# A 4x4 grid of convolution cells: the third of four copies of a last-column stream moves from VectorE to GpSimd

## What is computed

```python
def _cell(w, bias, ins):            # ins padded with zeros to 48 channels
    y = lax.conv_general_dilated(concatenate(ins, axis=1), w, (1, 1), 'SAME', ...)
    y = jax.nn.relu(y + bias[None, :, None, None])
    right, up, down = jnp.split(y, 3, axis=1)
    return (right, up, down)
for col in range(4):
    for row in range(4):
        if col == 0:   ins = [x] if row == 0 else [outs[row - 1][-1]]
        elif row == 0: ins = [outs[row][0], outs[row + 1][1]]
        elif row == 3: ins = [outs[row][0], outs[row - 1][-1]]
        else:          ins = [outs[row][0], outs[row + 1][1], outs[row - 1][-1]]
        outs[row] = _cell(W[col, row], b[col, row], ins)
return outs[-1][0]
x = x + grid(_gn(x), L0); x = x + conv(_gn(x)); x = x + gates(_gn(x)); x = x + grid(_gn(x), L3)
```

## Time and profile before

| | us |
|---|---|
| median of 3 runs | 434.03 (434.0 to 434.24) |
| the profiled execution, whole | 435.94 |
| its span, first to last instruction | 434.1 |
| PE busy | 403.1 (93%) |
| DVE busy | 301.6 (69%) |
| ACT busy | 199.4 (46%) |
| POOL busy | 205.2 (47%) |

### The profile page before, as it was taken

The page is one execution under the profiler, slowest core; times in us unless marked ns, Lnnn a source line. Parts: engine busy times, 40 slices in busy tenths (PEclk is TensorE's granted clock), DMA queues, the critical chain, the costliest instruction groups (busy, mean ns, idle before and its releaser), DMA issues.

```text
span 434.1 us, 12447 instructions
## 1 busy us (share of the span) xinstructions
PE 403.1 (93%) x5149; PEld 202.5 (47%) x5149; DVE 301.6 (69%) x563; ACT 199.4 (46%) x307; POOL 205.2 (47%) x384
## 2 busy tenths in 40 slices
PE   8999998989999897985998899999999999997884
PEld 5444444445554444543444455445444554444442
DVE  5789967537975346679587789968645954539684
ACT  7555533545526336465201455533545325347363
POOL 6277657955647433300000267657965594442300
PEclk9999999999999998999798999999999999998999
DMA  6076587868879665520000066588677797551701
GB/s 230 13 248 139 130 189 200 190 129 191 186 148 172 130 143 95 122 43 2 1 2 2 12 175 144 127 201 194 155 152 153 142 182 138 98 98 39 111 2 50
DMA packets 27304, 52.90 MB, mean 122 GB/s; under 512 B 11632, under 2 KB 13296, under 8 KB 27248
## 3 DMA queue, kind: packets, MB, share of 16 engines
q1 hardware_dynamic: 14416, 30.24, 30.8%
q0 software_dynamic: 12544, 21.14, 23.4%
q10 hardware_dynamic: 288, 0.72, 0.4%
HBM read 12.81 MB, written 0.52 MB: 31 GB/s over the span
## 4 chain that ended last, share of the span: by engine, by line
PE 57%; POOL 14%; DMA 11%; DVE 8%; ACT 5%; issue 3%; SPq 0%; DVEq 0%; ACTq 0%
PE bank L554 38%; PE bank L598 18%; POOL inp L534 11%; DMA inp<-cell_out 10%; POOL shifts L524 3%; ACT act_out L787 2%; DVE cell_out L1006 2%; DVE inp L718 1%; DVE inp L973 1%; DMA raw<-weights_in 1%; ACT cell_out L781 1%; ACT inp L718 1%; DVE inp L725 1%; DVE stat L860 1%; PE bank L617 1%
## 5 line engine op out<-in xcount | busy, mean ns | idle before, releaser
L534 POOL DMA_DIRECT2D inp<-cell_out x320 | 169.0, 536 | 142.1 <-DVE cell_out L1006 139.1
L787 ACT ACTIVATE act_out<-bank,bias 128x512 f32<-128x512 f32 x160 | 105.3, 687 | 101.3 <-PE bank L598 58.0
L554 PE MATMUL bank<-inp,w_heavy 128*32 128x512 f16 (+1 forms) x1536 | 139.8, 384 | 4.9 <-DMA inp<-cell_out 2.5
L1006 DVE TENSOR_TENSOR cell_out<-act_out,cell_out 128x512 f16<-128x512 f32 x156 | 107.8, 695 | 51.0 <-ACT act_out L787 47.0
L554 PE MATMUL bank<-inp,w_light 96*32 96x512 f16 (+2 forms) x1440 | 119.4, 395 | 12.8 <-DVE inp L973 10.3
L554 PEld LDWEIGHTS bank<-inp,w_heavy 128*32 128x32 f16 (+1 forms) x1536 | 65.1, 102 | 71.0 <-issue 13.8
L554 PEld LDWEIGHTS bank<-inp,w_light 96*32 96x32 f16 (+2 forms) x1440 | 59.8, 104 | 70.7 <-issue 19.8
L781 ACT ACTIVATE cell_out<-bank,bias 128x512 f16<-128x512 f32 x56 | 38.9, 694 | 87.0 <-PE bank L554 64.6
L598 PE MATMUL bank<-cell_out,w_first 32*128 32x512 f16 x1296 | 72.1, 378 | 0.0
L524 POOL DMA_DIRECT2D shifts<-inp x48 | 29.6, 623 | 59.0 <-DMA inp<-cell_out 58.8
L1000 DVE CAST cell_out<-act_out 128x512 f16<-128x512 f32 x100 | 42.9, 429 | 14.2 <-ACT act_out L787 13.5
(11 more groups left out here) (53 smaller groups left out, 170.1 us busy)
## 6 DMA issues: line engine op xcount, KB each, us to landing
inp<-cell_out SPq DMA_DIRECT2D x96, 72.2 KB, 3.6
inp<-cell_out SPq DMA_DIRECT2D x96, 71.2 KB, 3.8
raw<-weights_in SPq DMA_DIRECT2D x8, 672.0 KB, 5.0
inp<-cell_out POOLq DMA_DIRECT2D x128, 36.1 KB, 3.0
raw<-weights_in SPq DMA_DIRECT2D x8, 576.0 KB, 5.0
inp<-cell_out POOLq DMA_DIRECT2D x128, 35.1 KB, 3.2
shifts<-inp POOLq DMA_DIRECT2D x16, 144.5 KB, 3.1
inp<-cell_out POOLq DMA_DIRECT2D x32, 72.2 KB, 4.4
```

What stands on the lines that cost most here:

```text
L534: pool.dma_start(to, source).then_inc(signal, 16)
L554: last = pe.matmul(bank[j % BANKS][p:p + m, :], home[i][0:rows, w:w + m], source[:, off:off + PAIRS, dx:dx + SIDE], start=n == 0, stop=n = ...
L787: act.activation(act_out[:, n % T_RING, :], bank[j % BANKS][:, :], ACT.Relu, bias=bias[:, col + part[k]:col + part[k] + 1], scale=1.0 / W_ ...
L1006: dve.tensor_tensor(low, t, high, ALU.subtract).then_inc(cell_written, 1)
```

## The change

Image 2 of the copied stream goes to POOL: two images stay with DVE, one with ACT. POOL gets two semaphores of its own, and `copiers` has a third entry, so every consumer of the stream and every later writer of `cell_out` waits for POOL as well. The function `copier` is only moved up in the file so that the POOL block can use it.

```diff
-COPIED_BY = ("dve", "dve", "dve", "act")
+COPIED_BY = ("dve", "dve", "pool", "act")
...
+        pool_shift_done = sem("pool_shift_done")
+        pool_copied = sem("pool_copied")
...
-        copiers = {"dve": (dve_shift_done, dve_moved), "act": (act_shift_done, act_moved)}
+        copiers = {"dve": (dve_shift_done, dve_moved), "act": (act_shift_done, act_moved), "pool": (pool_shift_done, pool_copied)}
...
+            shift, even_rows = copier(pool, pool.tensor_copy, "pool")
             for st in cells:
+                if st in copied_before:
+                    shift(st, 0)
+                    even_rows(st, 0)
                 if st in shift_after:
                     move_shifts(shift_after[st])
                 last_k = -1
```

More of the change, by code:

```diff
@@ L462, in build, with copier, shift, even_rows @@
         block = ctx.enter_context(nc.Block())
+        def copier(eng, copy, name):
+            shift_done, done = copiers[name]
+            def shift(st, k):
+                if st in copied_before:
+                    eng.wait_ge(cell_written, emptied[jobs[st][k]][1])
+                    for (to, source), _ in copies(st, name):
+                        last = copy(to, source)
+                    last.then_inc(shift_done, 1)
+            def even_rows(st, k):
+                if st in copied_before:
+                    eng.wait_ge(shift_done, copied_before[st] + 1)
+                    for _, (to, source) in copies(st, name):
+                        last = copy(to, source)
+                    last.then_inc(done, 1)
+            return shift, even_rows
         @block.sync
@@ L708, in _ @@
                 grid_cell(st)
[L710 to L728, removed]
         @block.scalar
```

## The result

| | us |
|---|---|
| changed kernel, median of 4 runs | 446.29 (442.58 to 447.65) |
| kernel before, measured beside it, 4 runs | 434.01 (433.86 to 434.24) |
| ratio | 1.027 [1.021, 1.033] |
| profiled execution of the changed kernel, whole | 442.58 |
| its span | 440.8 |

What follows compares the result with a forecast made beforehand. PE, busy 93% of the span, was taken to be held up by gaps behind DVE's copies. Places 10.5 us plus clock 1.5 made 12.0 on 434.03: 446.0 us; forecast range 440 to 452, 8 in 10 reaching down to 431.0.

Steps and rivals of the forecast that it cites:

- Which gaps count: PE's gaps of 2.50, 1.10, 1.79 and 1.72 us in the second grid's last stretch; the change acts inside such gaps.
- DVE and POOL in turn: Copies of one cell: each engine waits out the other's copy, ending 3.9 us after L1006 against 2.79; chance 0.50.
- POOL's price: POOL's copies: 1.01 us for the shift, 1.07 for the even rows, from the long-row memset; upper bound together 3.4.
- POOL's late start: Start of POOL's copies: 0.29 us after the end of L1006, where DVE's copy begins 0.03 after it.
- A handover of 1.1 us: Before (3,2) of half 0 and (3,3): PE starts 1.1 us later, since the copies end later.
- (2,3) of half 1: Four POOL copies stand before this pack, so PE starts 2.1 us late, in each grid.
- The first grid's last cell: Before the sum into `res`: of the 1.1 us delay 0.8 is left, after 0.38 us of slack on DVE.
- The clock: PE's longer gaps bring one more stretch at granted clock 0.50 in all, costing 1.5 us.
- Side by side and faster: Rival: DVE and POOL don't hold each other up; handovers gain 2.75 us in all, 431.3 us; chance 0.22.
- Slow copies: Rival: side by side, but POOL's two copies take 3.4 us; PE starts 0.9 later in five handovers, 438; chance 0.12.
- POOL gets in only when DVE is idle: Rival: POOL's copies begin where DVE's end and DVE's next cell waits for them; 454 us or over; chance 0.07.
- What would show it: Profile marks: POOL COPY x12 rows, DVE copies over 1 us, new gap before (2,3), others grown 1.1, PE waiting for POOL.

Runs made afterwards that it cites:

- the first trace: The profiled execution of the changed kernel: 442.58 us whole, span 440.8 us.
- the filled kernel: Changed kernel with matmuls on zeros filling PE's gaps in the last stretches: 444.51 us, ratio 1.024.
- the filled pair: Kernel before and changed kernel, both with matmuls on zeros filling PE's gaps in the last stretches: 432.94 and 444.51 us.
- The repeated one: The changed kernel executed again without an edit: 445.14 us (440.42 to 448.75, 4 runs), ratio 1.024.
- the early pack: Kernel before with DVE's packs of (2,3) moved ahead of the low plane of (3,0): 434.38 us, ratio 1.001.

## Why the prediction was right, point by point

**Which gaps count.** Right. All that was lost in the touched stretches stands in the gaps of the earlier trace rows, one new gap, and the end of the span.

**DVE and POOL in turn.** Right, and it decided the sign. The reading of the earlier trace rows, a POOL access that waits out a DVE copy, was carried over to the other direction, which no row showed; DVE's greatest of 1239 ns shows it, and POOL beside DVE's three copies shows it without the rest of the change. The Trainium skill, SBUF — State Buffer, "Who interferes with whom", has the rule that the two engines' ports are locked for a whole instruction; the trace agrees, also for L1012 with two inputs, at 1.52 us. For a copy with one input the rule asks that VectorE be in a mode that uses both port pairs, which no row here shows by itself. By the records DVE's waiting shift ends 0.30 us after POOL's, where it takes 0.43 alone; whether 0.13 us of it really pass beside POOL's or POOL's recorded end is a little late stays open, since POOL's spans are rough in these profiles.

**POOL's price.** Right to 7%. POOL's shift takes 0.94 us from the end of DVE's first shift, its even rows 1.01 from the end of DVE's second, 0.86 to 0.87 ns an element in either, against 1.01 and 1.07 from the memset of the earlier trace rows. The choice of the near row over the far one was the step that mattered: this kernel shows 1.95 us for the two. The Trainium skill's GPSIMD Engine Reference, section 3.1, gives 1.8 cycles an element as the best case of an unrolled loop, an estimate of 3.4 us for the two, with which the trace doesn't agree; the same passage has 1.03 cycles an element for the smallest loop bodies (k of at most 2 there), an estimate of 1.93 us, with which it does. The prediction took up only the first of the two figures.

**POOL's late start.** Wrong, and it didn't matter. The 0.29 us of the earlier trace rows belong to issues of transfers; POOL's shift starts 0.06 behind the low plane and DVE's 0.03. Since the copies go in turn anyway, the start of the first is hidden behind DVE's shift.

**A handover of 1.1 us.** Right in kind, too large: 0.82 or 0.83, and 0.91 at one place, (3,2) of half 0 in the second grid of the first trace and of the filled kernel; where the extra 0.09 us come from stays open. Copies in turn cost 3.51 - 2.79 = 0.72, since POOL is 0.12 quicker and DVE's two waiting copies end 0.13 earlier each than whole copies behind POOL's would. To it come 0.10 for the third signal, which the prediction didn't have.

**(2,3) of half 1.** Predicted 2.1, measured 1.89 (the first matmul at T1+8.94 against T1+7.05 in the filled pair; with the handovers, 1.89 + 0.83 + 0.82 = 3.54 is the first grid's row T1 to T6), the one place where four POOL copies stand ahead of the pack. In the first trace each makes one DVE instruction wait about 0.8 us, where the prediction put the whole copy of 1.03 in line; and 4 x 0.81 less three DVE copies and the spaces between them, 1.37, gives 1.9. That the relief before (2,3) of half 0 is swallowed was right too: its gap went from 2.50 to 2.06, and the time didn't follow.

**The first grid's last cell.** Predicted 0.8, measured 0.37.

**The tail.** Missed: 1.18 us from POOL's closing instruction. What failed here isn't a term of the sum but its frame: it counted only work up to the last sum into `res`, and took the end of the span as fixed behind it. No row of before shows it, since there POOL's last issue ends 23 us before the last sum.

**The clock.** Predicted one more stretch at 1.5 us. The price is right where PE goes on without waiting for DVE (1.5 and 1.65) and wrong at the place where it was read, behind (2,3) of half 0, where it is 0.6 to 0.8. The number of stretches isn't fixed: the first trace has one more that costs, behind the gap of 1.92 before (3,2) of the first grid, and none behind the new gap, where it was forecast. (Another, behind the gap of 2.93 before (3,3) of half 0 there, costs nothing: T6 to R is 3.53 with and without it.) The repeated one has that one too and three in the second grid, at 399.8 (behind the new gap), 416.9 and 433.9, while it lacks the one at 394.3. Over the 9.55 us of the filled pair that makes +0.2 and +3.3 us for the two executions, net of the 1.4 us (0.83 + 0.61) that the kernel before loses to its own two stretches.

**The sum.** Places: predicted 10.5, measured 8.4 (3.54 + 0.37 + 3.64 + 0.82). Together with the tail 9.6, and with the clock 9.8 and 12.9 in the two traces. The medians say 12.3 and 12.0. So about 9.6 of some 12 us are shown by place, and the rest lies within what the clock does between executions; how much the clock takes in the median run can't be read from two traces and stays open. The sign and the size are earned; that 446.0 came within 0.3 of 446.3 is luck, from errors of opposite sign: places 2.1 us too large, the tail 1.2 too small and, if the rest is the clock, that 1.2 too small.

**The rivals.** Side by side and faster falls with the 1239 ns; even with the third copy left out altogether the gain is 0.7 to 1.1%. Slow copies fall with 0.94 and 1.01. That POOL gets in only when DVE is idle falls with the timeline: after each DVE copy POOL takes its turn, and DVE's next waits.

**What would show it.** Of the marks named, the twelve POOL rows, DVE's greatest over 1 us and the new gap came; the other gaps grew by 0.91, 0.53 and 0.82 (the second by 0.3 less than its handover, since (3,2) of half 1 in front of it started 0.3 later too). The one on PE waiting for POOL didn't: DVE is named.

## What to carry to other kernels

Before a copy is moved from VectorE to GpSimd, ask what VectorE does in the same microsecond: a small copy of 0.4 us that went to an engine needing 1.0 for it didn't run beside the others here but in the midst of them, and cost most of the difference (0.72 us for the two steps) although the slow engine had nothing else to do. The busy shares of the two engines don't tell this; a greatest duration far above the median on a line of the trace does (1054 against 487 ns before the change, 1239 against 436 after it). And when a long gap is closed, find out first what it covers: here the early pack gained nothing, since the transfers behind the gap were next.

## What the runs showed that I had not expected

- An engine that works late pays at the end: POOL's closing instruction takes 10.0 to 11.4 us and ends 9.9 us after its last copy or memset, and one memset of one element, 1.8 us before the last sum, lengthened the kernel by 4.5 us.
- A signal that came long ago costs its waiter 0.10 us if it stands behind the last one in the order of waits. With the last to arrive put last, the matmuls started 0.1 us earlier with two signals and 0.2 with three.
- The clock falls at different places in different executions of one kernel. Before (2,3) of half 0 in the second grid a gap of 2.06 us was followed by 0.50 in the first trace of the change, and one of 2.05 by 1.00 in the second. The places of such stretches make 3.1 us between these two traces, and a profile of one execution isn't enough to count them.
